# First batch of a residual attention block: eight landing slots, parameter loads on ScalarE's queue, and 20 pieces in place of 18 for VectorE

## The chip, the core and the metric

The kernel runs on one NeuronCore of a Trainium2 chip. The metric is the device time of the whole program in microseconds (us), as the median of three runs. Five engines work side by side, each on its own instruction stream, and meet at semaphores: TensorE (PE), VectorE (DVE), ScalarE (ACT), GpSimd (POOL) and SyncE (SP), which here only issues loads.

## The reference, cut to what matters

Input x is (4, 256, 128, 128) in float32. For each of the four batches:

```python
out = bilinear_resize(x, 64, 64)                  # two rows, then two columns, weighted
out = relu(bn(conv1x1(out, conv1_w), bn1))        # 256 -> 256 channels, 4096 pixels
q, k, v = conv1x1(out, q_w), conv1x1(out, k_w), conv1x1(out, v_w)   # 32, 32, 256
attn = softmax(q^T k)                             # 4096 x 4096
out = 0.5 * (v attn^T) + out
out = bn(conv1x1(relu(bn(out, bn2)), conv2_w), bn3)
y = relu(bilinear_resize(out, 128, 128) + x)
```

## The kernel before

**Stages.** A batch has a head and eight blocks. The head makes the small picture `a`, the queries `qs`, keys `ks` and values `vh`, `vl`, and the row maxima of the first query block. Each block then runs 512 queries against all 4096 keys, and beside it the picture of the next batch is shrunk and finished rows are enlarged, added to x and stored. The head of batch 0 has no block before it in which its picture could be shrunk, and the change lies there alone.

**Pieces.** The small picture is cut into eight chunks of 512 pixels. A chunk needs four pieces of x: 16 rows of the large picture as two times 8 rows, times two halves of the channels; a piece is 512 KB. In batch 0 the pieces are shared out. `V_OF` says how many of a chunk's four go to VectorE with ScalarE (V pieces, counted V0, V1, ...), and the rest go to GpSimd (P pieces, P0, P1, ...). Before, there are 18 V pieces and 14 P pieces.

- A V piece: ScalarE weights the rows in eight short activations (lines 498 and 499, `weight_rows`), VectorE then does five operations (lines 657 to 664, `first_down`). The weighted even rows stand in one of two PSUM banks, so the rows of piece i wait until VectorE has finished piece i - 2. The piece lands in slot i % 4 of `xres`, and its load waits until piece i - 4 is done.
- A P piece: six operations on GpSimd (lines 315 to 325, `down_piece`). It lands in one of two slots of `xin`, and its load waits until the P piece two before it is done.

All loads of x are issued by SyncE in the order of the picture, so a load that waits for its slot holds up every load behind it. Behind the first five pieces SyncE issues six loads of weights and then, on lines 242 to 250, fifteen small loads of parameters.

**Order of the head.** `SEQUENCE` is TensorE's order, `A_SEQUENCE` ScalarE's and `V_SEQUENCE` VectorE's. For chunk ck from 2 on, here called step ck, they are:

- TensorE: conv1 of chunk ck, first half; two products for row maxima (m0, m1) of the keys of chunk ck - 2; qk of chunk ck - 1; the product m2; conv1 of chunk ck, second half; m3. The maxima's products use two banks, so m1 waits until VectorE has reduced m3 of the step before, and m2 until it has reduced m0.
- ScalarE: rows of the first two V pieces of chunk ck + 2; eviction of conv1's first half (line 509); three evictions of qk of chunk ck - 1 (lines 517 to 519); rows of the third V piece of chunk ck + 2, where there is one; eviction of conv1's second half.
- VectorE: the V pieces of chunk ck + 2; maxima m0, m1, m2 (line 682); largest value of chunk ck - 1 (line 757) and the low parts of its keys and queries (lines 747 and 749); maximum m3.

Ahead of step 0 VectorE does the pieces of chunk 0, copies and scales the weights (`transposed_weights`, with `balance` in it, lines 603 to 645), scales the parameters (lines 672 to 677) and does the pieces of chunk 1. `balance` waits for all parameters.

Of the kernel before, what the change touches and what calls it, by code (L numbers as in the profile page):

```python
# [14 lines left out]
N = S * S  # L15
P = 128
# [19 lines left out]
BN = 1.0 / (1.0 + 1e-5) ** 0.5  # L36

DN, DV, UP = 6, 5, 5
V_OF = (3, 2, 3, 2, 2, 2, 2, 2)


def attention_block_kernel(nc, x, w1, s1, b1, wq, bq, wk, bk, wv, bv, gamma, s2, b2, w2, s3, b3,
                           ident_d, down_w, up_w, out):
    with ExitStack() as ctx:
# [6 lines left out]
        def sem(name):  # L51
            return ctx.enter_context(nc.semaphore(name))
# [62 lines left out]
        size_part, size_sum, even_step = sem("size_part"), sem("size_sum"), sem("even_step")  # L115
        xin_ld = [sem(f"xin_ld{i}") for i in range(2)]
        xres_ld = [sem(f"xres_ld{i}") for i in range(4)]
        stored = [sem(f"stored{i}") for i in range(4)]
        down_p, down_v, rows_w = sem("down_p"), sem("down_v"), sem("rows_w")
        up_p, up_v = sem("up_p"), sem("up_v")  # L120
# [92 lines left out]
            return PIECES * ck - v_before(ck)  # L213

        V_ALL, P_ALL = v_before(NB), p_before(NB)
        XRES_FIRST = [(V_ALL - s + 3) // 4 for s in range(4)]
        assert P_ALL % 2 == 0

        def down_count(b, d):

# [6 lines left out]
        @block.sync  # L227
        def _(sp):
            sp.dma_start(dw[:], down_w.partition_broadcast(P)).then_inc(dw_ld, 16)

            def load_weights():

                sp.dma_start(ident[:], ident_d).then_inc(wts_ld, 16)
                for dst, t in ((osb[:, 0:2, :], w1), (osb[:, 2:4, :], wv), (hbuf[:, :, 0:C], w2)):
                    sp.dma_start(dst, t.rearrange("(o p) c -> p o c", p=P)).then_inc(wts_ld, 16)
                sp.dma_start(hbuf[0:D, 0, C:2 * C], wk).then_inc(wts_ld, 16)
                sp.dma_start(hbuf[0:D, 1, C:2 * C], wq).then_inc(wts_ld, 16)

            def load_parameters():
                n = 0  # L240
                for i, t in ((S1, s1), (B1, b1), (S2, s2), (B2, b2), (S3, s3), (B3, b3), (BV, bv)):
                    sp.dma_start(par[:, i, :], t.rearrange("(h p) -> p h", p=P), allow_slow_non_contiguous=True).then_inc(par_ld, 16)
                    n += 1
                for i, t in enumerate((bk, bk, bq, bq)):
                    sp.dma_start(qkb[i * D:(i + 1) * D, :], t.unsqueeze(1)).then_inc(par_ld, 16)
                    n += 1
                sp.dma_start(gam[:], gamma.partition_broadcast(P)).then_inc(par_ld, 16)
                sp.dma_start(uw[:], up_w.partition_broadcast(P)).then_inc(par_ld, 16)
                for i, t in enumerate((bk, bq)):
                    sp.dma_start(wb[:, i:i + 1], t.unsqueeze(1)).then_inc(par_ld, 16)  # L250
                    n += 1
                assert n + 2 == N_PAR


            for d in (*FIRST_LOADS, *(d for d in range(NB * PIECES) if d not in FIRST_LOADS)):
                ck, j = divmod(d, PIECES)
                if d == FIRST_LOADS[-1]:
                    load_weights()
                    load_parameters()
                src = dram_rows(x, 0, j % 2, (2 * ck + j // 2) * DR, DR)  # L260
                if j < V_OF[ck]:
                    i = v_before(ck) + j
                    at_least(sp, down_v, DV * (i - 3))
                    sp.dma_start(xres[:, i % 4], src).then_inc(xres_ld[i % 4], 16)
                else:
                    i = p_before(ck) + j - V_OF[ck]
                    at_least(sp, down_p, DN * (i - 1))
                    sp.dma_start(xin[:, i % 2], src).then_inc(xin_ld[i % 2], 16)

            def load_shortcut(j, u, b, n, k):  # L270
                half, row = piece_rows(n, k)
                s = xslot(j)
                uses = (u - s) // 4 if isinstance(u, int) else None

                at_least(sp, stored[s], (u - s) * 4 if uses is None else uses * 16)
                if isinstance(u, int) and u < 4:
                    sp.wait_ge(down_v, DV * V_ALL)
                sp.dma_start(xres[:, s], dram_rows(x, b, half, row, UR)).then_inc(xres_ld[s], 16)

            def enter(b):  # L280
                pass

            def blk(b, n, c):
                ups = {j: (u, ub, un, k) for j, u, ub, un, _, k in up_pieces(b, n, c)}
                for j in range(PIECES):
                    if not (isinstance(b, int) and b == B - 1):

                        i = n * PIECES + j
                        sp.wait_ge(down_p, down_count(b + 1, i - 1))
                        sp.dma_start(xin[:, j % 2], dram_rows(x, b + 1, j % 2, (n * 2 + j // 2) * DR, DR)).then_inc(  # L290
                            xin_ld[j % 2], 16)
                    if j in ups:
                        load_shortcut(j, *ups[j])
                for j in range(PIECES, len(ups)):
                    load_shortcut(j, *ups[j])

            def leave(b):
                pass

            walk(enter, blk, leave)  # L300
            for u in range(LATE, PIECES * NB * B):
                j, ub, un, _, k = late_piece(u)
                load_shortcut(j, u, ub, un, k)
            for s in range(4):
                sp.wait_ge(stored[s], 16 * B * NB)
# [130 lines left out]
        def _(act):  # L436
            ops = nc.scalar

            def weights_of(s, t):

                act.wait_ge(et_rdy, s + 1)
                at_least(act, pv_done, s - 3)
                ops.activation(ph[:, t % 4, :], et[t % 2][:, :], ACT.Exp)  # L443
                ops.activation(et[t % 2][:, :], et[t % 2][:, :], ACT.Exp).then_inc(p_rdy, 1)  # L444
# [43 lines left out]
            def weight_rows(ck, js):  # L488

                for j in js:  # L490
                    i = v_before(ck) + j
                    x8 = xres[:, i % 4]
                    ev = weighted(i)
                    act.wait_ge(xres_ld[i % 4], 16 * (i // 4 + 1))
                    at_least(act, down_v, DV * (i - 1))
                    for r in range(DR // 2):
                        w = ((2 * ck + j // 2) * (DR // 2) + r) / (S - 1)
                        ops.activation(ev[:, r, :], x8[:, 2 * r, :], ACT.Copy, scale=1.0 - w)
                        last = ops.activation(x8[:, 2 * r + 1, :], x8[:, 2 * r + 1, :], ACT.Copy, scale=w)
                    last.then_inc(rows_w, 1)  # L500
# [99 lines left out]
        def _(dve):  # L600
# [46 lines left out]
            def first_down(ck):  # L647

                for j in range(V_OF[ck]):
                    i = v_before(ck) + j  # L650
                    odd = xres[:, i % 4].rearrange("p (r two) (c k) -> p r two c k", two=2, k=2)[:, :, 1]
                    ev = weighted(i).rearrange("p r (c k) -> p r c k", k=2)
                    right, step = rd[:, 0:DR // 2, :], rt[:, :, 0, :]
                    cw = dw[:, :].unsqueeze(1).broadcast_to([P, DR // 2, S])
# [570 lines left out]
```

## Time and profile before

| | us |
|---|---|
| median of three runs (lowest, highest) | 2481.05 (2480.34, 2482.93) |
| the profiled execution, its own time | 2478.03 |
| its span, first to last instruction | 2476.2 |
| busy in the span: TensorE | 2290.5 (92%) |
| VectorE | 1807.0 (73%) |
| ScalarE | 1800.5 (73%) |
| GpSimd | 1694.7 (68%) |

The shares are means over the whole span. In the first 100 us the picture is another one: TensorE is busy 6 of 10 us there, GpSimd over 9 of 10 from 40 us on. The first product of the first block starts at 146 us. Times in rows are counted from the start of the span.

### The profile page before, as it was taken

The numbers are of one execution on the slowest core, as the hardware profiler recorded it, in microseconds if no ns is written. First come the engines' busy times: TensorE is split into PE (matmuls) and PEld (weight loads), VectorE is DVE, ScalarE is ACT, GpSimd is POOL, SyncE is SP. The second block draws the span as 40 slices with busy tenths as digits, with TensorE's granted clock in tenths as the row PEclk, the third lists the DMA queues.
The fourth block names the chain that finished last, engine by engine and source line by source line (L and its number), as shares of the span: only waits on it lengthen the run. The fifth ranks groups of instructions, "written<-read, shape, count | busy, mean of one in ns | idle before, by whom it ended". The sixth has DMA issues, their size and how long they took to land.

```text
span 2476.2 us, 48184 instructions
## 1 busy us (share of the span) xinstructions
PE 2290.5 (92%) x15914; PEld 1636.0 (66%) x15914; DVE 1807.0 (73%) x3339; ACT 1800.5 (73%) x3345; POOL 1694.7 (68%) x1617
## 2 busy tenths in 40 slices
PE   4799999999999999999999999999999999999981
PEld 2377777777567777777747777777756777777760
DVE  7855577777777777777686777777777777777779
ACT  5467778877557787777747877887755778778762
POOL 7991088888548888888845888888853444444475
PEclk9899999999999999999999999999999999999995
DMA  6321022222102222222302222222310222111133
GB/s 206 100 77 35 1 76 102 102 94 102 51 26 95 94 102 102 102 93 98 108 1 78 95 93 102 102 102 93 106 39 18 69 69 68 68 60 63 64 103 136
DMA packets 59129, 204.11 MB, mean 82 GB/s; under 512 B 8736, under 2 KB 9824, under 8 KB 58976
## 3 DMA queue, kind: packets, MB, share of 16 engines
q1 hardware_dynamic: 40544, 135.26, 16.9%
q10 hardware_dynamic: 18432, 67.12, 6.6%
q8 instruction: 58, 0.95, 0.2%
q14 instruction: 95, 0.78, 0.1%
HBM read 135.24 MB, written 67.11 MB: 82 GB/s over the span
## 4 chain that ended last, share of the span: by engine, by line
PE 73%; DVE 15%; issue 5%; ACT 4%; POOL 3%; SPq 1%; DMA 0%; DVEq 0%; ACTq 0%; POOLq 0%
PE acc L1062 15%; PE acc L1064 14%; PE acc L1063 14%; PE et L940 8%; PE emx L928 5%; PE wrk L960 4%; PE acc L988 4%; DVE xres L740 4%; DVE xres L737 3%; DVE pl L710 3%; PE wrk L928 2%; PE acc L980 2%; ACT above L452 2%; PE wrk L952 1%; DVE am L757 1%
## 5 line engine op out<-in xcount | busy, mean ns | idle before, releaser
L1062 PE MATMUL acc<-vh,ph 128*128 128x257 f16 x4096 | 1120.5, 274 | 21.5 <-DVE pl L710 20.1
L1064 PE MATMUL acc<-vh,pl 128*128 128x257 f16 x4096 | 1116.2, 273 | 0.0
L1063 PE MATMUL acc<-vl,ph 128*128 128x256 f16 x4096 | 1111.0, 271 | 0.0
L710 DVE TENSOR_TENSOR pl<-et,ph 128x512 f16<-128x512 f32 x1024 | 701.6, 686 | 140.3 <-ACT et L444 135.7
L443 ACT ACTIVATE ph<-et 128x512 f16<-128x512 f32 x1024 | 610.5, 596 | 259.0 <-PE et L940 255.9
L444 ACT ACTIVATE et<-et 128x512 f32<-128x512 f32 x1024 | 608.9, 595 | 0.0
L1063 PEld LDWEIGHTS acc<-vl,ph 128*128 128x128 f16 x4096 | 401.1, 98 | 274.9 <-issue 20.5
L1062 PEld LDWEIGHTS acc<-vh,ph 128*128 128x128 f16 x4096 | 400.3, 98 | 95.5 <-DVE pl L710 26.7
L1064 PEld LDWEIGHTS acc<-vh,pl 128*128 128x128 f16 x4096 | 395.6, 97 | 56.1
L940 PE MATMUL et<-qs,ks 98*128 (+1 forms) x1024 | 390.3, 381 | 30.4 <-DVE pl L710 30.3
L352 POOL TENSOR_TENSOR ct<-cd,uw 128x512 f32<-128x512 f32 x248 | 317.7, 1302 | 79.3 <-DVE xres L740 73.0
L335 POOL TENSOR_TENSOR rd<-win 128x320 f32<-128x320 f32 x124 | 119.3, 962 | 318.0 <-ACT win L475 317.8
L689 DVE CUSTOM_DVE_ANT_0 above<-wrk,above 128x512 f32<-128x512 f32 x308 | 212.4, 690 | 146.4 <-PE wrk L928 95.2
L452 ACT ACTIVATE above<-emx 128x512 f32<-128x512 f32 x448 | 265.5, 593 | 39.0 <-PE emx L928 30.5
L345 POOL TENSOR_TENSOR y<-win,rt 128x512 f32<-128x512 f32 x124 | 170.1, 1372 | 174.6 <-DVE xres L737 167.2
L689 DVE CUSTOM_DVE_ANT_0 above<-emx,above 128x512 f32<-128x512 f32 x140 | 96.8, 692 | 220.5 <-PE emx L928 220.5
L737 DVE TENSOR_TENSOR xres<-xres,y 128x512 f32<-128x512 f32 x248 | 225.7, 921 | 4.3 <-POOL ct L352 4.3
L740 DVE TENSOR_TENSOR xres<-xres,ct 128x512 f32<-128x512 f32 x248 | 204.7, 836 | 0.0
L928 PE MATMUL emx<-kd,qm 96*128 96x512 f16 x448 | 171.0, 382 | 5.1 <-ACT above L452 4.9
L481 ACT ACTIVATE xres<-xres 128x1024 f32<-128x1024 f32 x128 | 134.1, 1048 | 50.6 <-DVE xres L740 50.5
L340 POOL TENSOR_TENSOR rt<-rd,uw 128x256 f32<-128x256 f32 x248 | 162.9, 678 | 9.7
L319 POOL TENSOR_TENSOR xin<-xin 128x512 f32<-128x512 f32 x110 | 146.7, 1334 | 8.6
(130 smaller groups left out, 2847.5 us busy)
## 6 DMA issues: line engine op xcount, KB each, us to landing
xres<-in_x SPq DMA_DIRECT2D x146, 512.0 KB, 4.5
out<-xres ACTq DMA_DIRECT2D x128, 512.0 KB, 2.6
xin<-in_x SPq DMA_DIRECT2D x110, 512.0 KB, 3.7
osb<-in_L_conv_conv_w SPq DMA_DIRECT2D x1, 256.0 KB, 7.6
osb<-in_L_conv_v_w SPq DMA_DIRECT2D x1, 256.0 KB, 7.6
hbuf<-in_L_conv_conv_w SPq DMA_DIRECT2D x1, 256.0 KB, 7.5
ident<-identity SPq DMA_DIRECT2D x1, 64.0 KB, 7.7
uw<-up_weights SPq DMA_DIRECT2D x1, 64.0 KB, 2.5
```

The lines of the kernel that those rows point to most:

```text
L352: last = ops.tensor_tensor(ct_[:, :, :, parity], cd_[:, :, parity:parity + S], wt, ALU.mult)
L443: ops.activation(ph[:, t % 4, :], et[t % 2][:, :], ACT.Exp)
L444: ops.activation(et[t % 2][:, :], et[t % 2][:, :], ACT.Exp).then_inc(p_rdy, 1)
L452: ops.activation(above[:, p % 2, :], (emx, wrk)[MAX_BANK[u]][:, :], ACT.Relu).then_inc(above_rdy, 1)
L689: ops.tensor_tensor_reduce(above[:, p % 2, :], (emx, wrk)[MAX_BANK[u]][:, :], above[:, p % 2, :], 1.0, LOWEST, ALU.add, ALU.max, mx[:, p % ...
L710: ops.tensor_tensor(pl[:, t % 4, :], et[t % 2][:, :], ph[:, t % 4, :], ALU.subtract).then_inc(pl_rdy, 1)
L740: ops.tensor_tensor(xs, xs, ct[:, rs].rearrange("p r c two -> p r (c two)"), ALU.add).then_inc(up_added, 1)
L928: mm(bank[:, :], qm[:, it * P:(it + 1) * P], keys, start=True, stop=True).then_inc(emx_rdy if taken else above_in, 1)
L940: mm(et[t % 2][:, :], ks[0:3 * D + 2, t * P:(t + 1) * P], qs[0:3 * D + 2, bass.ds(n * IB, IB)], start=True, stop=True).then_inc(et_rdy, 1)
L1062: mm(acc[it][:, 0:C + 1], ph[:, tt % 4, pt], vh[:, tt, 0:C + 1], start=tt == 0, stop=False)
L1063: mm(acc[it][:, 0:C], ph[:, tt % 4, pt], vl[:, tt, :], start=False, stop=False)
L1064: last = mm(acc[it][:, 0:C + 1], pl[:, tt % 4, pt], vh[:, tt, 0:C + 1], start=False, stop=tt == JT - 1)
```

## The change

Three things change, all in batch 0.

1. `V_OF` goes from (3, 2, 3, 2, 2, 2, 2, 2) to (3, 2, 3, 2, 3, 2, 3, 2). Chunks 4 and 6 now have three V pieces and one P piece: 20 V pieces, 12 P pieces.
2. V pieces land in eight slots: the four of `xres`, and four that borrow tiles which batch 0 does not use so early (`above`, `ct` and the last 1024 columns of either half of `a`). A V piece's load waits for piece i - 8 in place of i - 4.
3. The fifteen parameter loads are issued by ScalarE as the first thing it does, not by SyncE behind the weights.

```diff
-V_OF = (3, 2, 3, 2, 2, 2, 2, 2)
+V_OF = (3, 2, 3, 2, 3, 2, 3, 2)
+V_SLOTS = 8
...
-        XRES_FIRST = [(V_ALL - s + 3) // 4 for s in range(4)]
+        XRES_FIRST = [(V_ALL - s + V_SLOTS - 1) // V_SLOTS for s in range(4)]
...
+        def first_slot(i):
+
+            s = i % V_SLOTS
+            if s < 4:
+                return xres[:, s], xres_ld[s], 16 * (i // V_SLOTS + 1)
+            spare = (above[:].rearrange("p k (r c) -> p (k r) c", c=H), ct[:].rearrange("p r c two -> p r (c two)"),
+                     a[:, 0, N - 2 * IB:].rearrange("p (r c) -> p r c", c=H),
+                     a[:, 1, N - 2 * IB:].rearrange("p (r c) -> p r c", c=H))
+            return spare[s - 4], first_ld[s - 4], 16 * (i // V_SLOTS + 1)
...
                 if d == FIRST_LOADS[-1]:
                     load_weights()
-                    load_parameters()
...
                     i = v_before(ck) + j
-                    at_least(sp, down_v, DV * (i - 3))
-                    sp.dma_start(xres[:, i % 4], src).then_inc(xres_ld[i % 4], 16)
+                    slot, landed, _ = first_slot(i)
+                    at_least(sp, down_v, DV * (i - V_SLOTS + 1))
+                    sp.dma_start(slot, src).then_inc(landed, 16)
...
+            def load_parameters():
+                n = 0
+                for i, t in ((S1, s1), (B1, b1), (S2, s2), (B2, b2), (S3, s3), (B3, b3), (BV, bv)):
+                    act.dma_start(par[:, i, :], t.rearrange("(h p) -> p h", p=P), allow_slow_non_contiguous=True).then_inc(par_ld, 16)
+                    n += 1
...
+            load_parameters()
...
-                    x8 = xres[:, i % 4]
+                    x8, landed, count = first_slot(i)
                     ev = weighted(i)
-                    act.wait_ge(xres_ld[i % 4], 16 * (i // 4 + 1))
+                    act.wait_ge(landed, count)
```

**SyncE's queue**, from the last small loads before the pieces of chunk 1 on. Before:

```order
L250 DMA wb<-in_L_conv_q_b 32x1
L264 DMA xres<-in_x 128x1024
L264 DMA xres<-in_x 128x1024 [waits down_v]
L268 DMA xin<-in_x 128x1024 [waits down_p]
L264 DMA xres<-in_x 128x1024 [waits down_v] x3
L268 DMA xin<-in_x 128x1024 [waits down_p]
```

And in the changed kernel, from the last load of weights on:

```order
L249 DMA hbuf<-in_L_conv_q_w 32x256
L260 DMA xres<-in_x 128x1024
L260 DMA above<-in_x 128x1024
L264 DMA xin<-in_x 128x1024 [waits down_p]
L260 DMA ct<-in_x 128x1024
L260 DMA a<-in_x 128x1024 x2
L264 DMA xin<-in_x 128x1024 [waits down_p]
```

V3 to V7 no longer wait for a slot; `down_v` counts V pieces done, `down_p` P pieces.

**ScalarE in step 4**, where it evicts conv1 (`a<-acc`) and qk (`ks<-acc`, `qs<-acc`) and weights rows (`wrk<-xres`, `et<-xres`; each runs eight rows long, of which the first two stand). Before, the rows of both V pieces of chunk 6 stand ahead of the evictions, and after these comes step 5:

```order
L509 ACTIVATE a<-acc,par 128x512 [waits c1_rdy]
L517 ACTIVATE ks<-acc,qkb 64x512 [waits qk_rdy]
L518 ACTIVATE qs<-acc,qkb 64x512
L519 ACTIVATE qs<-acc,qkb 32x512
L509 ACTIVATE a<-acc,par 128x512 [waits c1_rdy]
```

In the changed kernel:

```order
L522 ACTIVATE a<-acc,par 128x512 [waits c1_rdy]
L530 ACTIVATE ks<-acc,qkb 64x512 [waits qk_rdy]
L531 ACTIVATE qs<-acc,qkb 64x512
L532 ACTIVATE qs<-acc,qkb 32x512
L511 ACTIVATE et<-xres 128x128 [waits down_v,xres_ld1]
L512 ACTIVATE xres<-xres 128x128
```

The rows of the third V piece of chunk 6 (V17) stand behind the evictions of qk. In step 2 it is the same with the third piece of chunk 4 (V12).

## Rows read from the trace of the kernel before

**Rows 1.** GpSimd in order of time: start, duration (us), idle before and its releaser

```profile
23.90 1.69 POOL L315 TENSOR_TENSOR xin<-xin 128x512 f32<-128x512 f32 x1 [3.78 <-DMA xin<-in_x]
35.32 1.27 POOL L315 TENSOR_TENSOR xin<-xin 128x512 f32<-128x512 f32 x1 [4.95 <-DMA xin<-in_x]
89.81 1.26 POOL L315 TENSOR_TENSOR xin<-xin 128x512 f32<-128x512 f32 x1
95.81 1.27 POOL L315 TENSOR_TENSOR xin<-xin 128x512 f32<-128x512 f32 x1
```

**Rows 2.** TensorE in order of time, conv1 of chunk 7, first half

```profile
101.98 1.95 PE L972 MATMUL acc<-xr,w1t 128*128 128x512 f32 x4 [1.13 <-POOL xr L325]
```

**Rows 3.** SyncE's queue in order of time, 8 to 31 us

```profile
8.24 0.43 SPq L242 DMA_DIRECT2D par<-in_L_conv_bn_s  x1
...
17.04 0.90 SPq L264 DMA_DIRECT2D xres<-in_x  x2
...
18.45 12.21 SPq L264 DMA_DIRECT2D xres<-in_x  x3
```

**Rows 4.** ScalarE in order of time, 0 to 70 us

```profile
0.74 1.28 ACT L498 ACT_TABLE_LOAD   x1 [0.74 <-PEq L1206]
6.64 0.28 ACT L498 ACTIVATE wrk<-xres 128x128 f32<-128x128 f32 x1 [4.62 <-DMA xres<-in_x]
...
52.55 0.68 ACT L517 ACTIVATE ks<-acc,qkb 64x512 f16<-64x512 f32 x1 [2.15 <-PE acc L980]
...
69.47 0.78 ACT L509 ACTIVATE a<-acc,par 128x512 f32<-128x512 f32 x1 [4.69 <-PE acc L972]
```

**Rows 5.** The line of ScalarE's own DMA issues: duration in ns, min, median, max

```profile
L486 ACTq DMA_DIRECT2D out<-xres x128: 337/338/374, 333.4 to 2473.1; - x128
```

**Rows 6.** VectorE in order of time, 8 to 31 us

```profile
8.45 0.43 DVE L657 TENSOR_TENSOR wrk<-xres,wrk 128x256 f32<-128x256 f32 x1 [5.46 <-ACT xres L499]
...
15.51 0.69 DVE L631 COPY w1t<-acc 128x512 f32<-128x512 f32 x1 [0.41 <-PE acc L884]
...
19.46 0.68 DVE L608 TENSOR_REDUCE ws<-hbuf 32x2 f32<-32x512 f32 x1 [1.55 <-DMA wb<-in_L_conv_q_b]
...
20.23 0.15 DVE L611 TENSOR_TENSOR ws<-ws,wb 32x2 f32<-32x2 f32 x1
...
26.91 1.17 DVE L675 TENSOR_TENSOR par<-par 128x2 f32<-128x2 f32 x1
...
28.18 0.42 DVE L657 TENSOR_TENSOR et<-xres,et 128x256 f32<-128x256 f32 x1
...
30.22 0.42 DVE L657 TENSOR_TENSOR wrk<-xres,wrk 128x256 f32<-128x256 f32 x1
```

**Rows 7.** VectorE in order of time, 44 to 119 us

```profile
44.19 1.21 DVE L757 TENSOR_REDUCE am<-a 128x2 f32<-128x1024 f32 x1
...
64.67 0.68 DVE L682 TENSOR_REDUCE mx<-emx 128x1 f32<-128x512 f32 x1
...
69.89 0.69 DVE L682 TENSOR_REDUCE mx<-et 128x1 f32<-128x512 f32 x1
...
89.59 0.68 DVE L682 TENSOR_REDUCE mx<-emx 128x1 f32<-128x512 f32 x1
...
96.80 0.69 DVE L682 TENSOR_REDUCE mx<-emx 128x1 f32<-128x512 f32 x1 [0.88 <-PE emx L906]
...
100.93 0.28 DVE L747 COPY ks<-ks 32x512 f16<-32x512 f16 x1
...
118.02 0.87 DVE L747 COPY ks<-ks 32x512 f16<-32x512 f16 x1 [0.53 <-ACT qs L519]
```

**Rows 8.** TensorE in order of time, 48 to 75 us

```profile
48.09 0.58 PE L906 MATMUL emx<-ks,qm 96*128 96x512 f16 x1 [4.08 <-DVE qm L714]
...
65.41 0.61 PE L906 MATMUL emx<-ks,qm 96*128 96x512 f16 x1 [4.65 <-DVE mx L682]
65.81 3.62 PE L972 MATMUL acc<-xr,w1t 128*128 128x512 f32 x4
...
72.41 1.88 PE L980 MATMUL acc<-a,wqk 128*128 128x512 f32 x4
```

**Rows 9.** Busy time in stretches: PE, PEld, DVE, ACT, POOL, granted clock, DMA share, GB/s

```profile
85.00:85.50 0.50, 0.36 (x1) 0.00 (x0) 0.50 (x2) 0.00 (x0) 0.42 (x2) 1.00 0.92 139
...
87.50:88.00 0.50, 0.00 (x0) 0.00 (x0) 0.45 (x2) 0.50 (x2) 0.42 (x2) 0.94 0.00 0
```

More of the change, by code:

```diff
@@ L117, in attention_block_kernel @@
         xres_ld = [sem(f"xres_ld{i}") for i in range(4)]
+        first_ld = [sem(f"first_ld{i}") for i in range(V_SLOTS - 4)]
         stored = [sem(f"stored{i}") for i in range(4)]
@@ L237, in load_weights @@
                 sp.dma_start(hbuf[0:D, 1, C:2 * C], wq).then_inc(wts_ld, 16)
[L239 to L252, printed above, removed]
             for d in (*FIRST_LOADS, *(d for d in range(NB * PIECES) if d not in FIRST_LOADS)):
@@ L437, in _ @@
             ops = nc.scalar
+            def load_parameters():
[3 more added lines that the diff above has]
+                    n += 1
+                for i, t in enumerate((bk, bk, bq, bq)):
+                    act.dma_start(qkb[i * D:(i + 1) * D, :], t.unsqueeze(1)).then_inc(par_ld, 16)
+                    n += 1
+                act.dma_start(gam[:], gamma.partition_broadcast(P)).then_inc(par_ld, 16)
+                act.dma_start(uw[:], up_w.partition_broadcast(P)).then_inc(par_ld, 16)
+                for i, t in enumerate((bk, bq)):
+                    act.dma_start(wb[:, i:i + 1], t.unsqueeze(1)).then_inc(par_ld, 16)
+                    n += 1
+                assert n + 2 == N_PAR
+            load_parameters()
             def weights_of(s, t):
@@ L650, in first_down @@
                     i = v_before(ck) + j
-                    odd = xres[:, i % 4].rearrange("p (r two) (c k) -> p r two c k", two=2, k=2)[:, :, 1]
+                    odd = first_slot(i)[0].rearrange("p (r two) (c k) -> p r two c k", two=2, k=2)[:, :, 1]
                     ev = weighted(i).rearrange("p r (c k) -> p r c k", k=2)
```

## The prediction, made before the changed kernel ran

> **What bounds the kernel now.** I read the chain of waits first, cut to the first 180 us, since nothing later is touched; then the timelines of GpSimd, SyncE, ScalarE, VectorE and TensorE over the same stretch, one after the other, and at the end the busy time in stretches of half a microsecond for TensorE's clock.
>
> The chain runs through GpSimd from 35 to 102 us. GpSimd stands still twice, 3.78 and 4.95 us, because a load has not landed, and from 35.32 us on it works without a gap: a P piece takes 6.0 us (starts at 89.81 and 95.81) [rows 1]. Both gaps come from SyncE: its queue is full of parameter loads until 17.04 us, and then the loads of V5 to V7 hold it for 12.21 us, waiting for slots [rows 3]. Conv1 of chunk 7 ends up 1.13 us late behind the last P piece [rows 2]. So GpSimd sets the pace of the head, and the change takes the right load off it. What counts is which chain comes second, and by how much.
>
> **GpSimd afterwards.** With P2's load free to go at 14.1 us (P0's end), and each later one when the piece two before is done, 6.0 us ahead of its use, both gaps go. Twelve pieces end near 8.1 + 12 x 6.0 = 80 us. Conv1 of chunk 7 needs the last one only after 100 us. GpSimd, 22 us faster, leaves the path altogether, and landing times could each be 1 us worse without a cost. The next path is VectorE with ScalarE and TensorE, and I follow it through by step, writing S2 to S6 for the start of m0 on VectorE in step 2 to 6. In the trace of before S6 is 96.80 [rows 7].
>
> **The start.** ScalarE must now issue 15 loads before its table load of 1.28 us and its first rows [rows 4]. SyncE took 17.04 - 8.24 = 8.8 us for them [rows 3]; ScalarE's own issues take 0.34 us, with gaps some 5.7 us for 15 [rows 5]. These are the two ends. The loads are the very ones of SyncE's rows, so I take 7.8. Then 0.7 + 7.8 + 1.28 = 9.8 us, and since V0's rows reach VectorE 8.45 - 6.64 = 1.8 us after they begin [rows 4, 6], VectorE's first piece starts at 11.6 in place of 8.45: 3.15 us late. Of this, VectorE had idle 0.41 and 1.55 us anyway, the latter waiting for the last parameter, which now comes early [rows 6]. That leaves +1.2 us (bounds 0 and +2.2).
>
> A second cost: in `balance` GpSimd stood still before (until 23.90) [rows 1], and now it runs through. The tiny operation of line 611 took 0.15 us in that quiet; a tiny one of the same kind on line 675, with GpSimd at work, took 1.17 [rows 6]. Lines 609, 611, 625 and 644 move from quiet into work: none to four of them times up to 1.0 us. I take +1.3 for the four, a third of the most (bounds 0 and +4).
> The Trainium skill, "SBUF — State Buffer", section "Who interferes with whom", says that a VectorE instruction with two inputs in SBUF, or in a two-port mode, and a GpSimd instruction that reads SBUF exclude each other for a whole instruction. The 1.17 us of line 675 agree. By that rule the gap removed from GpSimd is partly paid by VectorE; without it the +1.3 would be 0.
>
> So the pieces of chunk 1 start at 28.18 + 2.5 = 30.7. A piece is 30.22 - 28.18 = 2.04 us on VectorE [rows 6], and nothing is waited for by load any more: V3 to V9 take 7 x 2.04 and 0.3 for ScalarE's evictions in between, until 45.3 (before 44.19 [rows 7]). From there to m0's product on TensorE is 48.09 - 44.19 = 3.9 us [rows 7, 8]: 49.2.
>
> **Step 2, three V pieces.** V10 and V11 run from 49.2 to 53.3. V12 can't follow: its rows stand on ScalarE behind the evictions of qk of chunk 1. That qk stands behind m0 and m1 on TensorE. In the trace its eviction starts 52.55 - 48.09 = 4.46 us after m0 [rows 4, 8], three evictions take 2.1, the rows 1.7, the handoff 0.1: V12 starts at 57.5, ends at 59.5 = S2. VectorE idles 4.2 us. This is with TensorE at 1.2 GHz, as before in this place, where it had idled 4.08 us [rows 8]. At 2.4 GHz qk takes 1.88 instead of 3.6 us [rows 8] and S2 is 57.4.
>
> **A step of two V pieces** (pieces done in steps 3 and 5 follow the maxima of step 2 and 4). VectorE's own work from m0 to m3's end is 69.89 + 0.69 - 64.67 = 5.9 us [rows 7]. But the next piece's rows stand behind the eviction of conv1's second half, and that matmul waits for m0: m2's product comes 0.74 us after S, conv1 then takes 3.62 at 1.2 GHz, the eviction starts 4.8 after S (69.47 - 64.67) and takes 0.78, rows and handoff 1.8: the piece can start at S + 7.3 [rows 4, 7, 8]. Two pieces: 11.4 us. With 2.4 GHz it would be 5.9 + 4.1 = 10.0.
> **A step of three**: the third waits again for qk of the step. m1 waits for m3 at S + 5.9; with 2.4 GHz qk ends at S + 8.1, evictions S + 10.2, rows and handoff S + 11.9, piece S + 13.95. With 1.2 GHz conv1 and the rows ahead push it to 15.4. VectorE's own work is only 5.9 + 6.1 = 12.0.
>
> **Which clock where.** The clock fell 2.1 to 2.6 us after TensorE's last work at 85.36 [rows 9]; after that of 74.29 (72.41 + 1.88 [rows 8]) some 3.3 us went by. Steps 2 and 4 have idle of over 6 us ahead of m2, caused by the third piece: 1.2 GHz for sure. Steps 3 and 5 have 2.4 us: S plus 0.7 against qk's end at S - 1.9. I take 2.4 GHz there, and 1.2 GHz for qk of chunk 1 (2.6 us idle), where it was so before.
>
> **The sum.** S2 59.5; S3 +11.4 = 70.9; S4 +13.95 = 84.9; S5 +11.4 = 96.3; step 5 has no pieces behind it, 5.95 at full clock (before 96.80 - 89.59 = 7.2 [rows 7]): S6 = 102.2, against 96.80: +5.4 us. Behind it two small gains. The 1.13 us of conv1 of chunk 7 go [rows 2], but VectorE is then busy until 0.5 us of it: -0.5. The key copy at 118.02 took 0.87 with GpSimd at work and 0.28 at 100.93 in a gap [rows 7]; GpSimd is now idle there: -0.6. The rest of the head, to 146 us, is TensorE's own work and is moved as it is, like the blocks, which wait for it. Change: +4.3 us. The profiled execution took 2478.03 (span 2476.2), so one like it would take 2482.3; the median of the runs lies 3.02 above that execution, which gives 2485.3.
>
> **Rivals.**
> 1. *All at 1.2 GHz.* Step 3 costs 15.4 and step 5 7.2: +2.7 more, +7.0 in all, 2488.0. For it: every such step before was slow. Against it: their idle was 3.2 us or more, here 2.4. It decides from an idle in which the clock falls before conv1's second half. Slower, beyond what can be measured. Chance 0.25.
> 2. *Mostly at 2.4 GHz*, qk of chunk 1 too: S2 2.1 earlier, +2.2, 2483.2. Or the same from a start that costs nothing (+1.8). Chance 0.22.
> 3. *The third piece is covered.* If V12's and V17's rows were there in time, VectorE would bound alone: S2 = 49.2 + 6.1 = 55.3, then 10.0, 12.0, 10.0, 5.95: S6 = 93.3, -3.5, with the tail -4.6: 2476.4, and 2473.9 with a start that costs nothing. For it: GpSimd did set the pace, and 12 P pieces free 22 us. Against it: the order of ScalarE's rows stands in the listing. Chance 0.12.
> 4. *It doesn't do what it says*: the loads still come late, since ScalarE's small loads now share the way with V0, P0 and the weights. GpSimd has 20 us of slack, so only the start could feel it: up to +2 on V0, 2487.3. Chance 0.05.
> The Trainium skill, "DMA: Bandwidth & Descriptors", section "Issuing engines are not separate DMA queues", has all queues run on the same 16 engines and interleave, so that a second issuer saves issue time alone. No row here shows the two queues together at the start; by that rule case 4 has some weight, and ScalarE pays in issue time what SyncE saves.
>
> **Chances.** The forecast has 0.36. A measurement of this kernel can't tell a change under 0.2% (5.0 us) from none; the forecast of +4.3 lies just inside, and with the start's bounds two fifths of its chance fall beyond. Slower: 0.14 + 0.22 (rival 1, less its early-start part) + 0.04 = 0.40. Faster: a third-piece cover with a cheap start, and what I overlook: 0.11. Same: 0.49. Range: rivals 1 and 2 with their bounds, and the near edge of 3: 2478.0 to 2490.0.
>
> **What would show it.** Right: GpSimd's last P piece of batch 0 ends near 80 us; VectorE waits for ScalarE's rows ahead of V12 (4 us) and V17 (2 us), and about 1.4 us ahead of V13 and V18; S6 near 102. The start: V0 on VectorE near 11.6, line 657 of chunk 1 near 30.7. Wrong: no wait ahead of V12 (rival 3), S6 below 97, or ScalarE's issues over by 6.5 us. If the granted clock is 0.50 in conv1's second half of steps 3 and 5, rival 1 has it.

## The result, and the profile after

The changed kernel takes 2485.6 us (median of 22 runs, 2483.35 to 2490.58), the kernel before, run beside it, 2480.7 (22 runs, 2478.0 to 2483.0). The ratio is 1.0023 (95%: 1.0016 to 1.0029): slower by 0.2%, with 2485.3 forecast.

The profiled execution is one of the slowest of its runs: 2489.73 us, span 2487.9, where the one of before took 2478.03. So its trace shows a loss of 11.7 us where the medians show 4.9, and the steps below are read with that in mind.

**The start.** ScalarE's queue in order of time (start, duration, what, idle before and its releaser) begins with the parameter loads:

```profile
2.29 1.34 ACTq L438 DMA_DIRECT2D par<-in_L_conv_bn_b  x1
3.66 1.56 ACTq L438 DMA_DIRECT2D par<-in_L_conv_bn_s  x1
...
6.46 2.08 ACTq L441 DMA_DIRECT2D qkb<-in_L_conv_k_b  x2
...
11.50 1.28 ACT L511 ACT_TABLE_LOAD   x1 [11.50 <-issue]
```

Fifteen issues last from 0.75 to 11.47 us, 10.7 us; SyncE took 8.8 for them [rows 3]. Most take 0.5 us, three of the lines over 1 us for each load. Two of these stand where SyncE issues the first loads of x, which are slow as well: two took 3.04 us, where the same two at the same place took 0.91 before. The third (6.46) stands beside SyncE's loads of weights. SyncE is through with the weights at 9.70 us and issues V3 at once, where before it did so at 17.04; V6 and V7 follow at 16.41 without a wait:

```profile
2.11 3.04 SPq L260 DMA_DIRECT2D xres<-in_x  x2
...
9.74 0.42 SPq L260 DMA_DIRECT2D xres<-in_x  x1
```

VectorE in order of time, its first piece, the start of `balance`, some of its operations, the parameters' product and V3, to be held against [rows 6]:

```profile
14.61 0.43 DVE L670 TENSOR_TENSOR wrk<-xres,wrk 128x256 f32<-128x256 f32 x1 [11.62 <-ACT xres L512]
...
22.65 0.66 DVE L621 TENSOR_REDUCE ws<-hbuf 32x2 f32<-32x512 f32 x1
23.25 0.66 DVE L622 SCALAR_TENSOR_TENSOR wb<-wb 32x2 f32<-32x2 f32 x1
23.94 0.15 DVE L624 TENSOR_TENSOR ws<-ws,wb 32x2 f32<-32x2 f32 x1
...
26.04 0.72 DVE L638 TENSOR_SCALAR even_i<-even_i 128x2 int32<-128x2 int32 x1
...
28.04 1.27 DVE L657 SCALAR_TENSOR_TENSOR wva<-wvt 128x512 f32<-128x512 f32 x1
...
31.75 0.52 DVE L688 TENSOR_TENSOR par<-par 128x2 f32<-128x2 f32 x1
...
32.38 0.42 DVE L670 TENSOR_TENSOR et<-xres,et 128x256 f32<-128x256 f32 x1
```

The first piece is 6.2 us late (14.61 for 8.45), `balance` 3.2, V3 4.2. From `balance` to V3 it is 9.73 us, before 8.72.

Lines 609, 611, 625 and 644 of before are 622, 624, 638 and 657 here. Three of the four are longer than before, when GpSimd stood still:

```profile
20.06 0.14 DVE L609 SCALAR_TENSOR_TENSOR wb<-wb 32x2 f32<-32x2 f32 x1
...
22.32 0.17 DVE L625 TENSOR_SCALAR even_i<-even_i 128x2 int32<-128x2 int32 x1
...
23.78 0.69 DVE L644 SCALAR_TENSOR_TENSOR wva<-wvt 128x512 f32<-128x512 f32 x1
```

And these are the operations of GpSimd in the changed kernel beside which the three start:

```profile
22.86 1.04 POOL L313 TENSOR_TENSOR xin<-xin,dw 128x512 f32<-128x512 f32 x1
...
26.01 0.72 POOL L319 TENSOR_TENSOR dd<-dd,dw 128x256 f32<-128x256 f32 x1
27.50 1.26 POOL L311 TENSOR_TENSOR xin<-xin 128x512 f32<-128x512 f32 x1
```

The two short ones end at 23.91 and 26.76 us, just behind GpSimd's, which end at 23.90 and 26.73. The long one ends 0.55 us behind GpSimd's end at 28.76. Line 624 starts at 23.94, while GpSimd is between two operations (23.90 to 23.98), and takes 0.15 us as before.

**GpSimd** in order of time: its first piece, the last operation of the last P piece, and a wait behind it, which answer to [rows 1].

```profile
9.50 1.26 POOL L311 TENSOR_TENSOR xin<-xin 128x512 f32<-128x512 f32 x1 [3.96 <-DMA xin<-in_x]
...
81.31 0.74 POOL L321 TENSOR_TENSOR xr<-xin,dd 128x256 f32<-128x256 f32 x1
91.62 1.15 POOL L384 TENSOR_TENSOR kd<-ks 96x512 f16<-96x512 f16 x1 [3.59 <-DVE qs L762]
```

Both gaps are gone, the pieces are done at 82 us, and GpSimd then waits for VectorE, 3.59 us here and 12.88 at 110 us.

**The steps.** VectorE in order of time, the waits ahead of V12, V13 and V17 and m0 of steps 2 and 6 (S2 60.09, S3 71.36, S4 86.44, S5 97.72, S6 104.45), to be held against [rows 7]:

```profile
58.04 0.43 DVE L670 TENSOR_TENSOR wrk<-above,wrk 128x256 f32<-128x256 f32 x1 [3.36 <-ACT above L512]
60.09 0.68 DVE L695 TENSOR_REDUCE mx<-emx 128x1 f32<-128x512 f32 x1
...
67.28 0.43 DVE L670 TENSOR_TENSOR et<-ct,et 128x256 f32<-128x256 f32 x1 [0.93 <-ACT ct L512]
...
84.39 0.43 DVE L670 TENSOR_TENSOR et<-xres,et 128x256 f32<-128x256 f32 x1 [1.88 <-ACT xres L512]
...
104.45 0.69 DVE L695 TENSOR_REDUCE mx<-emx 128x1 f32<-128x512 f32 x1 [1.17 <-PE emx L919]
```

And TensorE at the same places, m2's product and conv1's second half of steps 2, 3 and 5, then the row of the softmax bound and qk of chunk 7, to be held against [rows 8]:

```profile
60.82 0.61 PE L919 MATMUL emx<-ks,qm 96*128 96x512 f16 x1 [6.75 <-DVE mx L695]
61.22 3.62 PE L985 MATMUL acc<-xr,w1t 128*128 128x512 f32 x4
...
72.11 0.60 PE L919 MATMUL emx<-ks,qm 96*128 96x512 f16 x1 [2.88 <-DVE mx L695]
72.50 3.40 PE L985 MATMUL acc<-xr,w1t 128*128 128x512 f32 x4
...
98.47 0.39 PE L919 MATMUL emx<-ks,qm 96*128 96x512 f16 x1 [2.41 <-DVE mx L695]
98.69 2.86 PE L985 MATMUL acc<-xr,w1t 128*128 128x512 f32 x4
...
120.47 1.87 PE L1029 MATMUL wrk<-wva,am 128*1 128x256 f32 x4 [1.06 <-DVE am L795]
122.27 3.78 PE L993 MATMUL acc<-a,wqk 128*128 128x512 f32 x4
```

At 1.2 GHz conv1's half takes 3.6 us, at 2.4 GHz 1.88; 3.40 and 2.86 are halves in which the clock changed. S6 comes 7.65 us later than before. The last two rows are a place that the prediction took as unmoved: the row of the softmax bound took 1.87 us and qk of chunk 7 behind it 3.78, both at 1.2 GHz (the granted clock from 120 to 126 us is 0.50); before they took 1.02 and 1.98. The first product of the first block starts at 155.72, before at 146.13: +9.6 us, and 2.1 us more are lost in the heads of batches 1 and 2. The medians show less than half of the sum.

### The profile page after: what moved, and what is told of

Read it like the earlier page. It is cut to its first block, busy times and chain, and to the rows that moved or that the text cites. A ratio compares the mean times of both kernels' runs of the same rounds, so it can differ in the third digit from the quotient of the medians.

```text
span 2487.9 us, 48200 instructions
## 1 busy us (share of the span) xinstructions
PE 2295.0 (92%) x15914; PEld 1637.5 (66%) x15914; DVE 1810.8 (73%) x3349; ACT 1803.6 (72%) x3361; POOL 1683.8 (68%) x1605
## 4 chain that ended last, share of the span: by engine, by line
PE 71%; DVE 16%; issue 5%; ACT 4%; POOL 3%; ACTq 0%; DVEq 0%; POOLq 0%
PE acc L1075 14%; PE acc L1077 14%; PE acc L1076 14%; PE et L953 8%; PE emx L941 5%; PE wrk L973 4%; PE acc L1001 4%; DVE xres L753 4%; DVE xres L750 3%; DVE pl L723 2%; PE wrk L941 2%; PE acc L993 2%; ACT above L465 2%; PE acc L985 1%; PE wrk L965 1%
```

## The experiments

The first eight kernels of these experiments ran 11 times each, with the kernel before beside them on the same chip. "Difference" is the median less that of before beside it, and by it kernels of different rows are compared; the ratio has its 95% interval, which is about 2 us to either side. S2, S6 and the first product of the first block are from the profiled execution.

| kernel | median | difference | ratio | S2 | S6 | block |
|---|---|---|---|---|---|---|
| before | 2480.7 | | | 52.27 | 96.80 | 146.13 |
| changed | 2485.6 | +4.9 | 1.0023 [1.0016, 1.0029] | 60.09 | 104.45 | 155.72 |
| eight slots alone | 2475.3 | -4.6 | 0.9982 [0.9973, 0.9991] | 50.89 | 89.99 | 141.91 |
| 20 pieces alone | 2485.1 | +5.7 | 1.0022 [1.0013, 1.0031] | 58.26 | 102.31 | 151.81 |
| parameters on ScalarE alone | 2480.9 | +1.5 | 1.0006 [0.9997, 1.0015] | 53.96 | 97.08 | 148.69 |
| slots and parameters | 2476.2 | -3.3 | 0.9984 [0.9974, 0.9993] | 54.41 | 90.33 | 139.53 |
| slots and 20 pieces | 2484.4 | +4.9 | 1.0017 [1.0008, 1.0026] | 57.46 | 101.74 | 153.01 |
| changed, third rows first | 2480.9 | +1.0 | 1.0004 [0.9995, 1.0013] | 56.32 | 98.45 | 148.60 |
| slots, 20 pieces, third rows first | 2476.5 | -3.4 | 0.9991 [0.9982, 1.0000] | 52.97 | 95.82 | 145.90 |
| slots, parameters behind V0 to V2 | 2477.0 | -2.8 | 0.9989 [0.9980, 0.9998] | 56.69 | 93.28 | 143.52 |

**18 pieces again**, in the changed kernel:

```diff
-V_OF = (3, 2, 3, 2, 3, 2, 3, 2)
+V_OF = (3, 2, 3, 2, 2, 2, 2, 2)
```

> The changed kernel with the split of before (18 V pieces, 14 P pieces); eight slots and parameter loads on ScalarE stay. My theory: the start costs 4.2 us as in the changed kernel (first piece of chunk 1 near 32.4), and the two stalls for the third piece (3.4 and 1.9 us) and 4.1 us of VectorE's work go. Then VectorE's steps of 11.3 us each follow from m0 near 54.7: S6 near 95 (104.5 in the changed kernel, 96.8 before), GpSimd's last P piece near 94. Total 2 to 4 us under the kernel before, so 7 to 9 under the changed one. Rival one, all of the loss is the start: S6 stays 4 above before, total +4. Rival two, crowding of loads by eight slots: first pieces' landing and GpSimd's gaps would show it, total +3 or more.

Measured 2476.20, 3.3 us under before, so 8.2 under the changed kernel by the differences: both as expected. The way there was another one: S6 is 90.33, not near 95, since the steps take 9.8 us and not 11.3. VectorE and TensorE in step 3 and 4, in order of time:

```profile
64.27 0.68 DVE L695 TENSOR_REDUCE mx<-emx 128x1 f32<-128x512 f32 x1
...
69.94 0.43 DVE L670 TENSOR_TENSOR wrk<-a,wrk 128x256 f32<-128x256 f32 x1
...
74.03 0.68 DVE L695 TENSOR_REDUCE mx<-emx 128x1 f32<-128x512 f32 x1
```

```profile
65.01 0.39 PE L919 MATMUL emx<-ks,qm 96*128 96x512 f16 x1 [2.69 <-DVE mx L695]
65.24 1.88 PE L985 MATMUL acc<-xr,w1t 128*128 128x512 f32 x4
```

A two-piece step takes 9.8 us, no piece waits for its rows, and conv1 runs at full clock, though TensorE's idle (2.69 us) is longer than the 2.41 us ahead of the slowed 98.69 of the changed kernel. Two steps later the same idle in the same kernel is followed by a slowed half:

```profile
84.45 0.61 PE L919 MATMUL emx<-ks,qm 96*128 96x512 f16 x1 [2.69 <-DVE mx L695]
84.85 3.29 PE L985 MATMUL acc<-xr,w1t 128*128 128x512 f32 x4
```

The two-piece steps take 11.3 us in the changed kernel, so the third piece goes with a loss in the steps beside its own too.

**The parameter loads back on SyncE**, in the changed kernel: `load_parameters` is taken out of ScalarE's stream and issued by SyncE behind `load_weights`, as before.

> The changed kernel with the parameter loads back in SyncE's queue behind the weights; 20 V pieces and eight slots stay. My theory: ScalarE starts its first rows near 6.6 instead of 12.8, chunk 1's first piece is at 28.2 to 28.5 instead of 32.4, GpSimd's gap near 20 to 24 us comes back and costs nothing. S2 near 56, S6 near 100. Total 4 us less than the changed kernel, +0.5 to +1.5 against before. Rival, the start is absorbed later and all the loss is the third piece: same total as the changed kernel, +5.

Measured 2484.40, +4.9 us, as the changed kernel. V3 starts at 28.14 in place of 32.38, S2 only 2.6 us earlier, because the wait ahead of V12 grows from 3.36 to 4.35 us: its rows stand behind qk, which ran wholly at 1.2 GHz. Of the 4.2 us of the start nothing is seen at the end here, as the rival had it; the expected gain of 4 us didn't come.

**20 pieces alone**, in the kernel before: the one line of `V_OF`.

> The kernel before with the new split alone (20 V, 12 P pieces; four slots, parameters on SyncE). My theory: third pieces stall as in the changed kernel (V12 waits some 3.5 us for its rows, V17 some 2), GpSimd ends near 90 and is off the path, S6 near 101, total +1 to +3. Rival, relieving GpSimd pays as long as ScalarE's queue is left alone: total -3 to -6.

Measured 2485.12, +5.7 us. The waits ahead of V12 and V17 are there (4.01 and 1.88), in four slots as in eight. With this and the other corners each part has a price: the split costs 5.7 us alone, 9.5 with slots, 8.2 with slots and parameters; slots give 4.6 alone and 0.7 with the split. VectorE's stalls and GpSimd's relief are both in this kernel, and the stalls win, by more than the +1 to +3 us expected; the rival's gain is refuted.

**The parameters on ScalarE alone**, in the kernel before: only the fifteen loads move.

> The kernel before with only the parameter loads moved to ScalarE. My theory: the start is 4.2 us later on VectorE (chunk 1 near 32.4), the loads of V5 to V7 wait for VectorE's pieces of chunk 0 and 1 with four slots, so P3's load is late by the same and the chain through GpSimd shifts: last P piece near 106, total +4. Rival, GpSimd's chain gains from SyncE's freer queue (P2 starts at 20 and not at 23.9): total -2 to 0.

Measured 2480.93, +1.5 us, its interval reaching 1, between the +4 expected and the rival's 0. GpSimd's last P piece ends at 103.1 us, not near 106. From `balance` to V3 VectorE needed only 6.53 us here, so V3 was 1.2 us late and not 4.2. VectorE and GpSimd in order of time:

```profile
27.28 0.73 DVE L644 SCALAR_TENSOR_TENSOR wva<-wvt 128x512 f32<-128x512 f32 x1
...
29.07 0.16 DVE L675 TENSOR_TENSOR par<-par 128x2 f32<-128x2 f32 x1
```

```profile
27.54 1.06 POOL L308 TENSOR_TENSOR xr<-xin,dd 128x256 f32<-128x256 f32 x1
```

GpSimd is done at 28.60 and then idle for 8.40 us, waiting for a load: the parameters' operation that took 1.17 us in [rows 6] takes 0.16.

**The third piece's rows ahead of qk's evictions**, in the changed kernel, on ScalarE alone:

```diff
-                            weight_rows(i // 2 + 2, js[2:] if i % 2 else js[:2])
+                            weight_rows(i // 2 + 2, js[:0] if i % 2 else js[:2])
                         conv1_out(b, i // 2, i % 2)
+                        if is_first(b) and i % 2 == 0 and i // 2 + 2 < NB:
+                            weight_rows(i // 2 + 2, js[2:])
```

> The changed kernel, with the rows of a third V piece weighted ahead of the evictions of qk (behind the eviction of conv1's first half). My theory: V12 and V17 no longer wait 3.4 and 1.9 us, S2 comes at 56.7 instead of 60.1, and TensorE's idle in step 2 shrinks from 6.8 to some 3.3 us. S6 at 97 to 99 (104.5 in the changed kernel); total 5 to 8 us under the changed kernel, 0 to 3 under the one before. Rival, the loss is VectorE's own work in two more pieces (4.1 us) and the start: no more than 2 us gained.

Measured 2480.87, +1.0 us where the changed kernel has +4.9, and level with before. The gain of 3.9 us lies between the 5 to 8 expected and the rival's 2. VectorE and then TensorE, in order of time:

```profile
54.28 0.42 DVE L672 TENSOR_TENSOR wrk<-above,wrk 128x256 f32<-128x256 f32 x1
56.32 0.68 DVE L697 TENSOR_REDUCE mx<-emx 128x1 f32<-128x512 f32 x1
```

```profile
68.35 0.39 PE L921 MATMUL emx<-ks,qm 96*128 96x512 f16 x1 [2.13 <-DVE mx L697]
68.58 1.88 PE L987 MATMUL acc<-xr,w1t 128*128 128x512 f32 x4
```

V12 follows V11 without a wait, S2 comes at 56.32 (56.7 expected), and the three-piece step, all at full clock, takes 11.8 us (67.61 to 79.39) in place of 15.1. The two-piece steps still take 11.3 and 11.1 us, with waits of 1.17 and 1.21 us ahead of V13 and V18, so the loss in the steps beside a third piece stays without the waits ahead of V12 and V17, and what makes it isn't shown.

**The same with the parameters on SyncE:**

> As the last, and the parameter loads back in SyncE's queue: 20 V pieces, eight slots. My theory: the start gives another 2.6 to 4.2 us as between the changed kernel and the one with only the loads moved back: S6 at 93 to 96, total 3 to 6 us under the kernel before. Rival, the start's gain is lost to TensorE's clock as it was there: equal to the last.

Measured 2476.52, -3.4 us, with S6 at 95.82, both as expected, where the same with the third rows behind qk has +4.9. So with the parameters on SyncE the place of one piece's rows on ScalarE, in two steps, accounts for 8.3 of the split's 9.5 us, with the parameters on ScalarE for 3.9 of 8.2. Each of these is uncertain by some 3 us, and why the second is the smaller one isn't shown. Even with the rows first, 20 pieces are no faster than 18: -3.4 beside the -4.6 of slots alone, +1.0 beside -3.3.

**Eight slots alone**, in the kernel before: `V_SLOTS = 8` and `first_slot`, nothing else.

> The kernel before with eight slots alone (18 V pieces, parameters on SyncE). My theory: GpSimd keeps its gap near 20 to 24 us, since P2's load is behind the parameters, and loses the second one; 14 P pieces then end near 97 (101.8 before, 93.9 with the loads on ScalarE), and GpSimd sets the pace again. Total 2 to 4 us under the kernel before, about as the kernel with loads on ScalarE and 18 pieces. Rival, VectorE sets the pace: its start is 4.2 us earlier than there, total 6 to 7 under before.

Measured 2475.31 (2473.55 to 2477.28), the lowest median of all, 4.6 under before where 2 to 4 were expected. GpSimd keeps its first gap (3.85 us) and loses the second, and its last P piece ends at 96.3 us. It still sets the end of this head, as TensorE shows at conv1 of chunk 7:

```profile
96.42 1.96 PE L984 MATMUL acc<-xr,w1t 128*128 128x512 f32 x4 [2.38 <-POOL xr L337]
```

**The parameters behind the rows of V0 to V2**, with 18 pieces and slots, to keep VectorE's first pieces early:

```diff
-            load_parameters()
...
-            for ck in range(2):
-                weight_rows(ck, range(V_OF[ck]))
+            weight_rows(0, range(V_OF[0]))
+            load_parameters()
+            weight_rows(1, range(V_OF[1]))
```

> The changed kernel with 18 V pieces, and ScalarE issues the parameter loads behind the rows of V0 to V2, in place of ahead of them. My theory: the first rows start near 6.6 again, the loads are issued from 12.3 to 19 or 20, the last lands near 22, so VectorE's balance starts near 22 at the latest, as when they were first (22.6); gain 0 to 2 us on the start, total 3 to 5 under the kernel before. Rival, issue is quicker once the queues are idle (0.38 us each, 5.7 in all): balance near 20.5, gain 2.

Measured 2477.04, -2.8 us, where the loads at the front have -3.3. The piece V0 starts at 8.93, but the last load is issued at 19.01 and VectorE stands 7 us for it, until 6.65 us behind the start of that issue (before: 2.89 us, 16.57 to 19.46). The expectation had 22 us for this place:

```profile
25.66 0.67 DVE L620 TENSOR_REDUCE ws<-hbuf 32x2 f32<-32x512 f32 x1 [7.13 <-DMA wb<-in_L_conv_q_b]
```

Most issues took 0.49 us, the fifteen 8.0 us in all (11.51 to 19.52). SyncE issues four loads of x in this time, and neither queue is slowed by the other to speak of, as one load of ScalarE and two of SyncE show (ScalarE's two at 15.09 take 0.56 us each):

```profile
14.57 0.49 ACTq L438 DMA_DIRECT2D par<-in_L_conv_v_b  x1
```

```profile
15.43 0.93 SPq L260 DMA_DIRECT2D a<-in_x  x2
```

**Conv1's second half ahead of m2.** The last four runs have 5 executions each, and 9 of the kernel before beside them (median 2481.41). In TensorE's order, for all four heads:

```diff
-        seq += ... else first + m[:2] + middle + m[2:3] + second + m[3:]
+        seq += ... else first + m[:2] + middle + second + m[2:]
```

> The changed kernel, with one edit in TensorE's order, in every head: conv1's second half of chunk ck stands ahead of the product m2, so that it no longer waits for VectorE's m0. Theory (the third piece costs through TensorE: it stands idle for 7 us ahead of m2, and conv1's second half then runs at 1.2 GHz and late, which holds up the rows of the next pieces): conv1's second half takes 1.88 us behind qk in steps 2 to 5, the waits ahead of V13 (0.93), V15 (0.74) and V18 (1.28) go, the waits ahead of V12 (3.4) and V17 (1.9) stay, since qk's place is the same. A two-piece step falls from 11.3 to about 9.9, the three-piece step from 15.1 to about 13.9; S6 near 100 in place of 104.45, the time about 4 us less than the changed kernel: 2481 to 2482 beside a kernel before of 2480. Rival (the waits for rows and VectorE's own work set it, TensorE's clock is only a sign): S6 at 103 or later, time within 1.5 us of the changed kernel.

Measured 2542.09, ratio 1.0261 [1.0235, 1.0287]: as a total, both expectations failed, by 55 us or more. In the head of batch 0 the theory held up to S6. VectorE in order of time:

```profile
56.62 0.43 DVE L670 TENSOR_TENSOR wrk<-above,wrk 128x256 f32<-128x256 f32 x1 [2.22 <-ACT above L512]
...
80.53 0.43 DVE L670 TENSOR_TENSOR et<-xres,et 128x256 f32<-128x256 f32 x1 [1.92 <-ACT xres L512]
...
98.30 0.68 DVE L695 TENSOR_REDUCE mx<-emx 128x1 f32<-128x512 f32 x1
102.52 0.69 DVE L695 TENSOR_REDUCE mx<-emx 128x1 f32<-128x512 f32 x1 [2.94 <-PE emx L919]
```

The waits ahead of V13, V15 and V18 are gone, those ahead of V12 and V17 stand; the two-piece steps take 9.9 and 10.2 us and the three-piece step 14.0 (S2 58.66, S3 68.56, S4 82.58, S5 92.82), and S6 is 98.30, 6.15 us earlier. But m2 now comes later, VectorE makes the low parts of keys behind it, and the next product of maxima waits for these. From step 6 on this takes the gain back (m2 waits 2.94 us there), the block starts only 1.7 us earlier (154.04), and the heads of batches 1 to 3, which had next to no such wait, pay in full. TensorE in the head of batch 1, first in the changed kernel and then here:

```profile
668.70 0.60 PE L919 MATMUL et<-ks,qm 96*128 96x512 f16 x2 [0.20 <-DVE qs L762]
```

```profile
668.59 0.60 PE L919 MATMUL et<-ks,qm 96*128 96x512 f16 x2 [1.89 <-DVE qs L762]
```

In that head the waits ahead of the maxima's products come to 12.9 us, in the changed kernel to 2.7. Four of its eight qk take 2.7 to 3.5 us, where all but the last took 1.88. From the last product of a block to the first of the next, the head takes 104.7 us, in the changed kernel 88.0; the heads of batches 2 and 3 take 105.0 and 102.0, in the changed kernel 88.1 and 86.0.

> As the run before, with the parameter loads back on SyncE's queue. Theory: 1 to 3 us less than the run before it, since VectorE starts its first pieces 4 us earlier: 2479 to 2480. Rival (the late start is given back elsewhere): the same time within 1 us.

Measured 2539.57: 2.5 us less than with the loads on ScalarE, in the direction expected, the intervals overlapping; as a total, 60 us over the expectation, by the later heads. S6 is 94.69, 3.6 earlier.

> The kernel before, with eight slots, 18 V pieces, the parameter loads on SyncE's queue, and conv1's second half ahead of m2. Theory: steps 4 and 5 fall from 12.2 and 6.7 to 9.9 and 6, but GpSimd's last P piece still ends near 96 and conv1 of chunk 7 can't be earlier: time within 1 us of eight slots alone, 2475 to 2476; the wait of conv1 of chunk 7 for GpSimd grows from 2.4 to over 5 us. Rival (GpSimd is not the bound there): 3 us less, 2472.

Measured 2531.68, 56 us over the expectation. S6 is 90.44, no earlier than with slots alone, and the total suffers from the later heads as above (102.4 us for the head of batch 1). Steps 4 and 5 fall to 10.1 and 6.3 us, as expected, but the step behind S2 grows from 9.9 to 12.2. GpSimd's last P piece ends at 96.4 us, and conv1 of chunk 7 waits for it 0.16 us, not over 5, since it now comes later itself. Which of the two views of GpSimd holds isn't told by it.

> 20 V pieces, eight slots, the parameter loads on SyncE's queue, the third piece's rows ahead of the evictions of qk, and conv1's second half ahead of m2. Theory: nothing on ScalarE or TensorE holds up VectorE, which bounds alone: S2 52.9, two-piece steps 9.9, three-piece 11.9, the last 6: S6 near 90.6, and conv1 of chunk 7 doesn't wait for GpSimd, whose last piece ends near 84. 2471 to 2473, the lowest of all. Rival (TensorE's clock falls at another place and takes it back): 2475 to 2477, as eight slots alone.

Measured 2533.27, 60 us over the expectation. S2 is 52.97 as forecast, S6 91.45 for 90.6, and again m2 waits behind it (4.40 us) and the later heads lose. An order for batch 0 alone wasn't tried. Of what was run, eight slots alone has the lowest median; slots with the parameters moved, and slots with 20 pieces and the third rows first, lie within the noise of it.

## Why the prediction was right

The total came within 0.3 us, and the mechanism is the one named: GpSimd leaves the path, and the third piece's rows, late on ScalarE, hold up VectorE. That it is so close is luck in part. The change itself was +4.9 us for a forecast +4.3, uncertain by 1.6, and several terms were off. In the profiled execution they don't cancel: for one like the profiled one of before the forecast was 2482.3, and this one took 2489.73.

- **GpSimd off the path: right.** Done at 82 us (80 forecast; the first piece's load landed 1.4 us later than before), both gaps gone. That it gains nothing on the whole: right for the changed kernel. But the reason is sharper than I put it: the slots alone pay 4.6 us, and the split takes all of it and 5 more.
- **The start: mis-sized.** I took 7.8 us for ScalarE's issues, with 8.8 as the upper bound; it was 10.7 (2.9 over). V0 came at 14.61, not 11.6, and `balance` 3.2 us late, not 1.2. The bound was a row in which one queue issues alone. It was also no fixed price: with the loads issued from 11.51 us on, the same fifteen took 8.0. By the Trainium skill, "DMA: Bandwidth & Descriptors", section "Issuing engines are not separate DMA queues", a second issuer saves only issue time; the trace agrees: SyncE issues V3 at 9.74 us in place of 17.04, and ScalarE pays 10.7 us for it. As for the price of the late start, kernels with and without it differ by 1.5 (alone), 1.3 (with slots), 0 (slots and split) and 4.4 us (third rows first as well), each uncertain by some 3. Their mean is 1.8, where the forecast charged 2.5; which of the four differ in truth stays open.
- **Collisions, +1.3: right in size and in mechanism, save for the row that stood for it.** The stretch grew by 1.0 us. Of the four operations named, line 611's stayed at 0.15 us, and the others grew by 0.52, 0.55 and 0.58, 1.65 in all. The operations behind them gave some back: the one of line 675, 1.17 us before, took 0.52. By the Trainium skill, "SBUF — State Buffer", section "Who interferes with whom", whole instructions exclude each other. The traces agree: the operations of 0.66 and 0.72 us end when GpSimd's does, and so does line 675 before (28.08 us, GpSimd at 28.06). So how long each waits hangs on how much of GpSimd's operation is left when it starts, and the count of operations gives no more than a bound. With the parameters alone on ScalarE the whole stretch took 6.5 us with GpSimd at work until 28.60.
- **Step 2: right.** V12 waited 3.36 us (4.2 forecast, with qk at 1.2 GHz; it ran partly at the higher clock, 3.02 us), S2 was 60.09 for 59.5, of which the start alone is 1.7. With the rows first, rival 3's condition is met: it priced that at 8.9 us (-4.6 for +4.3). Measured were 8.3 with the parameters on SyncE, and 3.9 in the changed kernel, where the two-piece steps kept their 11.3 and 11.1 us for the rival's 10.0.
- **Two-piece steps, 11.4: the forecast number, at a cost of clock.** 11.3, with waits of 0.93, 0.74 and 1.28 us for rows (1.4 forecast). I had placed 2.4 GHz in step 3; conv1's second half ran there mostly at 1.2 (3.40 us; granted clock 0.50 until 74.0 us), so from S3 to S4 it took 15.1, not 13.95, near rival 1's 15.4. In step 5 that half took 2.86 us. By the sign set for rival 1, 0.50 in both halves, it has most of step 3 and part of step 5 in this execution. I judged the clock by the idle time just ahead. That failed both ways: 2.88 and 2.41 us were followed by slowed halves in the changed kernel, 2.69 us by full clock with 18 pieces. What the rows do show is that the changed kernel, with two waits of 7 us, has none of the steps 2 to 5 wholly at full clock, and the one with slots and parameters, without such waits, has three from S2 on. In the traces of these kernels with conv1 in its old place, idles of 4 us and more ahead of m2 were all followed by a slowed half; those of 2.1 to 3.0 us six times by full clock and eight times not.
- **Step 5, 5.95: too low.** It took 6.7, conv1's halves partly at 1.2 GHz (2.86 and 2.42 us).
- **"The rest of the head is moved as it is": wrong.** In the profiled execution qk of chunk 7 ran at 1.2 GHz (3.78 for 1.98 us), like the product ahead of it (1.87 for 1.02), and VectorE waited 3.81 us behind qk where it had waited 1.81. Together that is some 3 us, and it is no fixed cost. In the first ten kernels qk takes 3.6 to 3.8 us there in the changed kernel, in slots alone, in slots with 20 pieces and in slots with the parameters behind V0 to V2; it takes 1.98 in before, in 20 pieces alone and in slots with parameters, and 2.6 to 3.0 in the other three. The head of batch 1 has the same place: 88.0 us in the changed kernel, 86.3 before. Both places may have gone better in the runs nearer the median; that wasn't traced. The key copy of chunk 7 did fall from 0.87 to 0.28 us, as forecast, but that of chunk 6 rose from 0.88 to 1.22.

Why the sum still came out: S6 was 2.3 us later than forecast (start 1.7, clock in step 3 1.1, step 5 0.8, less 1.3 by step 2 and the two-piece steps), in an execution 4.1 us over its median. Behind S6, up to the first product of the block, it lost another 1.9 us where 1.1 were to be gained. At the median the forecast fits; the traces can't show which of its terms were smaller in the other runs, and that stays open.

## What to carry to other kernels

Taking work from the engine that bounds pays only if the engine that gets it is not held by the order of a third one: here eight short activations, put behind three evictions, made the difference between -3.4 and +4.9 us. An engine that TensorE waits for can cost twice, once by the wait and once by the clock of the matmuls after it: TensorE's idles of 4 us and more ahead of m2 were all followed by a slowed half, shorter ones went either way. And before reordering one engine, look which loops share the order: an edit that gave 6 us up to S6 of one head cost 16 to 17 in each of three others.

## What was not expected of the hardware

- The price of an issue is not fixed. In the first 8 us, beside SyncE's first loads, ScalarE's small loads took up to 1.56 us each, and two of SyncE's loads of x 3.04 us, where SyncE by itself took 0.91 for them. From 11.51 us on ScalarE's took 0.49 each, and at 15 us, where both queues issue at once, they took 0.56 and SyncE's 0.47. SyncE by itself had slow ones too, as one small load of 1.20 us at 9.80 before. So two queues at once are not enough to explain it, and what is stays open. ScalarE's own large stores take 0.34 [rows 5].
- TensorE idles 2.69 us and keeps 2.4 GHz in two steps of one kernel, idles 2.69 us and drops two steps later in the same one. The idle just before a matmul doesn't tell its clock.
- VectorE's stretch from `balance` to V3 took 6.5, 8.7 and 9.7 us in three kernels, with the same operations and GpSimd at work for half of it or more each time. The operation of line 675, 0.16 us by itself, took 0.52 or 1.17 beside one of GpSimd's, and ended with it both times; those of 128 x 1 elements (line 623, 0.15) were not held beside GpSimd.
